# A row sort in which GpSimd makes a sixth of the upper payload words

## The reference

```python
idx = jnp.argsort(vf, axis=-1)                  # 3136 values of each channel
vs = jnp.take_along_axis(vf, idx, axis=-1)
gat = lambda t: jnp.take_along_axis(t.reshape(b, c, hw), idx, axis=-1)
out1 = _reshape_attn(gat(q1), gat(k1), vs, temperature, True)
out2 = _reshape_attn(gat(q2), gat(k2), vs, temperature, False)
inv = jnp.argsort(idx, axis=-1)
out1 = jnp.take_along_axis(out1, inv, axis=-1)  # and out2
```

## Time and profile before

| | us |
|---|---|
| median of 3 runs | 15142.0 (15140.57 to 15142.44) |
| the profiled execution | 15131.19 |
| its span | 15129.3 |
| VectorE busy | 13763.9 (91%) |
| ScalarE busy | 7104.4 (47%) |
| TensorE busy | 6739.8 (45%) |
| GpSimd busy | 6003.8 (40%) |

### The profile page before, as it was taken

One profiled execution on the slowest core, in us unless ns is written; L12 is line 12 of the kernel. 1 busy time (PEld: TensorE's weight loads), 2 busy tenths in 40 slices (PEclk: granted clock), 3 DMA queues, 4 the chain that ended last, 5 costly groups with the idle time before them and its releaser, 6 DMA issues. The chain is left out here.

```text
span 15129.3 us, 121619 instructions
## 1 busy us (share of the span) xinstructions
PE 6739.8 (45%) x42188; PEld 2753.7 (18%) x42188; DVE 13763.9 (91%) x8241; ACT 7104.4 (47%) x6587; POOL 6003.8 (40%) x4372
## 2 busy tenths in 40 slices
PE   4777744481025625714814723833732015433310
PEld 2443421120012211211201211211211002111100
DVE  4777778899999999999999999999999999989978
ACT  0000003355575565565565566566566555444443
POOL 0000000066666666666666666666666640000000
PEclk8888877795557857856956966966866557666655
DMA  1554553110001000100100100100100001221232
GB/s 33 123 134 109 131 118 76 55 43 13 12 12 35 27 12 30 32 12 30 31 12 26 36 12 23 38 12 12 45 17 12 33 29 53 84 66 54 77 76 66
DMA packets 343162, 699.24 MB, mean 46 GB/s; under 512 B 71581, under 2 KB 275582, under 8 KB 331702
## 3 DMA queue, kind: packets, MB, share of 16 engines
q1 hardware_dynamic: 342518, 691.17, 17.1%
HBM read 480.98 MB, written 209.95 MB: 46 GB/s over the span
## 5 line engine op out<-in xcount | busy, mean ns | idle before, releaser
L1183 DVE COPY_PREDICATED arena<-psum,arena 128x4096 f32<-128x4096 uint32 (+26 forms) x1456 | 4009.6, 2771 | 46.4 <-ACT psum L1143 45.8
L1190 DVE COPY_PREDICATED arena<-psum,arena 128x4096 f32<-128x4096 uint32 (+26 forms) x1456 | 3969.2, 2742 | 42.0
L1009 PE MATMUL psum<-arena,wt 128*32 128x448 f32 x31360 | 3224.9, 573 | 1239.5 <-DMA arena<-xpad 698.8
L1108 POOL TENSOR_TENSOR arena<-arena 128x1024 int32<-128x1024 int32 (+26 forms) x1456 | 2077.7, 1433 | 3061.6 <-DVE arena L1175 3058.2
L1094 POOL TENSOR_TENSOR arena<-arena 128x1024 bf16<-128x1024 f32 (+26 forms) x1456 | 1975.6, 1363 | 3284.0 <-SPq L267 3081.3
L1131 ACT ACTIVATE arena<-arena 128x4096 f32<-128x4096 f32 (+26 forms) x1456 | 3071.7, 2126 | 71.1 <-DVE arena L1190 38.0
L1151 ACT ACTIVATE masks<-psum 128x512 fp8e4<-128x512 f32 (+27 forms) x1256 | 923.6, 736 | 3563.6 <-DVE arena L1190 3562.5
L1100 POOL TENSOR_TENSOR arena<-arena 128x1024 int32<-128x1024 int32 (+26 forms) x1456 | 2006.1, 1384 | 0.0
L1009 PEld LDWEIGHTS psum<-arena,wt 128*32 128x32 f32 x31360 | 1039.5, 115 | 3427.5 <-issue 2326.4
L1399 PE MATMUL psum<-ident,arena 128*112 128x128 f32 x896 | 197.1, 386 | 2443.1 <-ACT arena L1318 1879.8
L1175 DVE TENSOR_TENSOR arena<-arena 128x1024 f32<-128x1024 f32 (+26 forms) x1456 | 1163.4, 812 | 100.4 <-POOL arena L1100 100.4
(11 more groups left out here) (131 smaller groups left out, 7837.8 us busy)
## 6 DMA issues: line engine op xcount, KB each, us to landing
arena<-xpad SPq DMA_DIRECT2D x896, 108.5 KB, 2.3
arena<-simd SPq DMA_DIRECT2D x416, 210.0 KB, 4.3
arena<-simd SPq DMA_DIRECT2D x416, 196.0 KB, 4.4
xpad<-arena SPq DMA_DIRECT2D x8, 1924.0 KB, 14.6
arena<-in_x SPq DMA_DIRECT2D x8, 1568.0 KB, 7.3
x3d<-arena SPq DMA_DIRECT2D x8, 1568.0 KB, 5.3
prodd<-arena SPq DMA_DIRECT2D x8, 1568.0 KB, 5.1
arena<-prodd SPq DMA_DIRECT2D x8, 1568.0 KB, 14.0
```

Of the source, the lines that this page charges most:

```text
L1009: last = nc.tensor.matmul(psum[C * b:C * b + C, n % C_BANKS, 0:CROWS * W], wt[:, g, C * w:C * w + C], cx[i % 2][b][:, y0:y0 + CROWS, x0:x0 ...
L1108: last = nc.gpsimd.tensor_tensor(hi, packed_view(stmp, here, piece, 1), lo, ALU.subtract)
L1183: last = nc.vector.copy_predicated(lo, wide_mask(q, k, piece, here), hi)
L1190: last = nc.vector.copy_predicated(hi, wide_mask(q, k, piece, here), packed_view(ptmp, here, piece, NP))
```

## The change

A share (POOL_SHARE = 0.16) of the pairs of each lot is cut off at its upper end (`cut_piece`, `shared_lot`), at a boundary of a block, of a run or of 8 elements where one is within a sixteenth of the lot. The table SHARED holds for each level and lot the pieces kept and the pieces given. For the kept ones all stays as it was. For the given ones:

- GpSimd forms the integer sum of the lower and upper payload words into `ptmp` (`pay_sums`), ahead of the masked copy, and afterwards writes the upper words as that sum less the new lower ones (`pay_uppers`).
- ScalarE's `keep_pay` and VectorE's `upper` leave them out. VectorE's `lower` still covers all pairs.

New waits: `pay_sums` waits for `upper` and `pay_uppers` of the level before, `pay_uppers` for the lot's `lower`, `keep_pay` for `pay_uppers` of the level before, `lower` for `pay_sums`. GpSimd's order is written anew: difference and sum of a level are made one level ahead, lot by lot, behind the upper keys of the same lot; only at LAST_LEVEL both lots wait until the level before is through.

```diff
+POOL_SHARE = 0.16
+def cut_piece(piece, x, slack):
+    base, nb, sb, j0, ng, sg, w, d = piece
+    block, n = ng * w, size(piece)
+    for unit in (block, w, 8, 1):
+        if w % unit and unit < w:
+            continue
+        c = min(n, max(0, round(x / unit) * unit))
+        if abs(c - x) <= slack:
+            break
...
+def shared_lot(rows):
+    total = sum(size(piece) for piece, _ in rows)
+    x, slack = total * (1 - POOL_SHARE), total / 16
+    kept, given = [], []
+    for piece, _ in rows:
+        low, high = cut_piece(piece, min(size(piece), max(0, x)), slack)
+        kept += low
+        given += high
+        x -= size(piece)
+    return kept, given
...
+            def pay_sums(q, k):
+                if q:
+                    pool.wait_ge(d_hi[k], q)
+                    pool.wait_ge(k_pu[k], q)
+                    if k or q == LAST_LEVEL:
+                        pool.wait_ge(d_hi[1 - k], q)
+                        pool.wait_ge(k_pu[1 - k], q)
+                for piece, here in shared_rows(q, k, 1):
+                    lo, hi = pair_views(pay[b].bitcast(i32), piece, NP)
+                    last = nc.gpsimd.tensor_tensor(packed_view(ptmp.bitcast(i32), here, piece, NP), lo, hi, ALU.add)
+                last.then_inc(k_ps[k], 1)
+
+            def pay_uppers(q, k):
+                pool.wait_ge(k_ps[k], q + 1)
+                pool.wait_ge(d_lo[k], q + 1)
+                for piece, here in shared_rows(q, k, 1):
+                    lo, hi = pair_views(pay[b].bitcast(i32), piece, NP)
+                    last = nc.gpsimd.tensor_tensor(hi, packed_view(ptmp.bitcast(i32), here, piece, NP), lo, ALU.subtract)
+                last.then_inc(k_pu[k], 1)
+
+            def prepare(q, k):
+                differ(q, k)
+                sums(q, k)
+
+            for k in range(2):
+                prepare(0, k)
+                pay_sums(0, k)
             for q in range(SR):
-                if q == LAST_LEVEL:
-                    uppers(q - 1, 1)
-                differ(q, 0)
-                sums(q, 0)
-                if q and q != LAST_LEVEL:
-                    uppers(q - 1, 1)
-                differ(q, 1)
-                sums(q, 1)
-                uppers(q, 0)
-            uppers(SR - 1, 1)
+                ahead = q + 1 < SR and q + 1 != LAST_LEVEL
+                for k in range(2):
+                    uppers(q, k)
+                    if ahead:
+                        prepare(q + 1, k)
+                    pay_uppers(q, k)
+                    if ahead:
+                        pay_sums(q + 1, k)
+                if q + 1 == LAST_LEVEL:
+                    for k in range(2):
+                        prepare(q + 1, k)
+                        pay_sums(q + 1, k)
...
             def keep_pay(q, k):
                 if q:
                     act.wait_ge(d_hi[k], q)
+                    act.wait_ge(k_pu[k], q)
                     if k or q == LAST_LEVEL:
                         act.wait_ge(d_hi[1 - k], q)
-                for piece, _, here in lot_rows(q, k):
+                        act.wait_ge(k_pu[1 - k], q)
+                for piece, here in shared_rows(q, k, 0):
...
             def lower(q, k):
                 dve.wait_ge(d_cp[k], q + 1)
+                dve.wait_ge(k_ps[k], q + 1)
                 dve.wait_ge(d_mw[k], q + 1)
...
             def upper(q, k):
                 dve.wait_ge(d_lo[k], q + 1)
-                for piece, _, here in lot_rows(q, k):
+                for piece, here in shared_rows(q, k, 0):
```

More of the change, by code:

```diff
@@ L179, with group @@
 assert all(lot_size(q, 0) <= lot_at(q, 1) for q in range(len(ROW_LOTS)))
+POOL_SHARE = 0.16
[8 more added lines that the diff above has]
+            break
+    b, rest = divmod(c, block)
+    g, i = divmod(rest, w)
+    low, high = [], []
+    def group(into, lo, hi):
+        if lo < hi:
+            into.append((base + b * sb, 1, sb, j0 + g * sg + lo, 1, 0, hi - lo, d))
+    if b:
+        low.append((base, b, sb, j0, ng, sg, w, d))
+    if g:
+        low.append((base + b * sb, 1, sb, j0, g, sg, w, d))
+    group(low, 0, i)
+    if i:
+        group(high, i, w)
+    first = g + (i > 0)
+    if rest and first < ng:
+        high.append((base + b * sb, 1, sb, j0 + first * sg, ng - first, sg, w, d))
+    done = b + (rest > 0)
+    if done < nb:
+        high.append((base + done * sb, nb - done, sb, j0, ng, sg, w, d))
+    assert sum(map(size, low)) == c and sum(map(size, low + high)) == n
+    return low, high
+def shared_lot(rows):
[8 more added lines that the diff above has]
+    return kept, given
+SHARED = [[shared_lot(rows) for rows in lots] for lots in ROW_LOTS]
 for q, (first, second) in enumerate(ROW_LOTS):
+    assert all(kept and given for kept, given in SHARED[q])
     assert sum(size(x) for x, _ in first + second) == ROW_NET[q][2]
@@ L1029, in c_scalar @@
                         yield
-        k_df, k_sm, k_up = ([sem(f"k_{n}{k}") for k in range(2)] for n in ("df", "sm", "up"))
+        k_df, k_sm, k_up, k_ps, k_pu = ([sem(f"k_{n}{k}") for k in range(2)] for n in ("df", "sm", "up", "ps", "pu"))
         d_mw, d_mcp, d_cp, d_lo, d_hi = ([sem(f"d_{n}{k}") for k in range(2)] for n in ("mw", "mcp", "cp", "lo", "hi"))
@@ L1035, in program @@
         d_mst = [sem(f"d_mst{i}") for i in range(4)]
-        d_sems = [*k_df, *k_sm, *k_up, *d_mw, *d_mcp, *d_cp, *d_lo, *d_hi, *d_lv, *d_mst]
+        d_sems = [*k_df, *k_sm, *k_up, *k_ps, *k_pu, *d_mw, *d_mcp, *d_cp, *d_lo, *d_hi, *d_lv, *d_mst]
         pmask = psum[:, 4:8, :].rearrange("p k n -> p (k n)")
@@ L1043, in lot_rows, with shared_rows @@
                 yield piece, at, here
+                here += size(piece)
+        def shared_rows(q, k, part):
+            kept, given = SHARED[q][k]
+            here = lot_at(q, k) + (sum(map(size, kept)) if part else 0)
+            for piece in (kept, given)[part]:
+                yield piece, here
                 here += size(piece)
```

## The result

The changed kernel takes 15766.8 us in the median of 4 runs (15764.8 to 15768.1), the kernel before beside it 15142.2 (15140.6 to 15143.1): the ratio is 1.0414, with a 95% interval of 1.0397 to 1.0430. It is 625 us slower; the forecast was 15,790. The profiled execution took 15764.8 us, its span is 15762.9.

A forecast was written before the change was run, and what follows sets the result against it. GpSimd was to replace VectorE as the bound: 1082 work + 44 handovers + 100 and 6 port - 9 overlap + 25 edges = 1248 us per sort against 1166.6, so 650 us slower: 15,790 us, range 15,370 to 16,080.

The forecast's parts named there:

- What goes away: VectorE's upper payload copies lose 66,308 words per sort: 69 us per sort, 550 us in eight sorts.
- GpSimd's new operations: Two integer payload operations per given piece, 356 per sort at 0.98 us each: 349 us per sort.
- The port: SBUF access shared by GpSimd and VectorE's two-input operations: GpSimd loses 100 us per sort to key minima, 6 to attention.
- The handovers: GpSimd operations waiting for the subtraction before them: two per lot at 0.14 us, 44 us per sort.
- The edges: GpSimd idle at each sort's start, at LAST_LEVEL and in the last level: together 25 us per sort.
- The whole: GpSimd's total need per sort: 1248 us, against 1166.6 us per sort before the change.
- Rival 1: VectorE stays the bound, paying for the port, with payload words at 1.67 ns: near 15,440 us; chance 0.20.
- Rival 4: Met waits cost 0.14 us each and minima take the port for their full 1.21 us: near 16,340; chance 0.06.
- The new wait of ScalarE: ScalarE's payload copy waits for GpSimd's payload subtraction, holding back mask words queued behind it: given no cost.
- VectorE's slices: Sign in the profile after: VectorE's busy tenths per slice in the sorts fall from 9 to 8.
- rival 2: The two engines don't hinder each other when loaded: 15,015 us, or 14,590 with cheap payload words; together chance 0.08.
- The rule of the Trainium skill: Whichever engine starts first keeps the shared ports for the whole instruction, 1.21 us per minimum: sum about 190 us higher.

The follow-up runs named there:

- the run without payload work: Changed kernel with all waits and order kept, but GpSimd's payload sums and subtractions left out: 14598.0 us, ratio 0.9640.
- the run with one input: Changed kernel with the key minimum replaced by an in-place reduction over one element, reading one arena operand, so nothing is sorted: 15107.9 us, ratio 0.9979.
- the run with the mask words first: Changed kernel with ScalarE's mask words written ahead of its payload copy in each lot: 15745.3 us, ratio 1.0401.
- the share of 0.12: Changed kernel with a share of 0.12 instead of 0.16 and nothing else: 15429.0 us, ratio 1.0191.
- 0.08: Changed kernel with a share of 0.08 instead of 0.16: 15111.7 us, ratio 0.9983.
- the masked key copy with 0.12: Changed kernel with the key minimum made a copy under the PSUM mask, mask words ahead of ScalarE's payload copy, share 0.12: 15068.6 us, ratio 0.9954.

## Why the prediction was right

The forecast and the result differ by 23 us, and it is right by its steps, not only by its sum. GpSimd's needs per sort are, in the sum and as measured, 1082 and 1082 us of work, 44 and 40 of handovers, 97 and 91 of the port (the attention's 6 lie in the measured 1082), 25 and 34 of edges and waits. That the differences of -4, -6 and +9 cancel is luck, but a small one:

- **What goes away:** 550 us by the sum, 543 by the run without payload work (565 by the upper copies' group, of the changed kernel).
- **GpSimd's new operations:** 0.98 us each in the sum, 0.991 and 0.989 in the run with one input, 351 us per sort by that run ((1404.3 + 1400.9)/8) for 349. With the key operations GpSimd is busy for 8656.04/8 = 1082 us per sort there, overlapping records counted once:

```profile
3021.00:12328.00 9307.00, 3977.61 (x30128) 1475.96 (x30128) 8559.15 (x4964) 5114.76 (x5088) 8656.04 (x7216) 0.70 0.07 23
```

- **The port:** 100 us per sort for the key minima, 6 for the attention's operations, less 9. The one-input run shows 91 for the key minima, from GpSimd's side; the attention's part is in both runs and not in this difference. Its two-input operation (L1468, L1373 before) takes 1285 ns in the one-input run and 711 in the kernel before, so it too meets the port. The forecast of VectorE's side was loose ("1.2 us and more" for the mean; 1.37).
- **The handovers:** 44 us per sort in the sum. What GpSimd's idle time before the differences and the payload sums has left, once what the waits name is taken off, is 3245.8 - 3058.0 - 27.1 = 161 us (27.1 us is named as issue among its waits) and 252.3 - 94.4 = 158 us, together 40 us per sort.
- **The edges and GpSimd's other waits:** 25 us in the sum. The stretch has 1247 us per sort, GpSimd is busy for 1173, and less the 40 the rest is 34. Of these 25 are the waits for VectorE that the groups name ((84.6 + 94.4 + 23.8)/8).
- **The whole:** 1248 us per sort, 1247 measured.

Rival 1, VectorE as the bound with cheap payload words, fell with the price of a payload operation: 0.99 us and not 0.80 (0.18 us + 372 x 1.67 ns). Rival 4, at 16,340, needed another 44 us of handovers and 24 of the port per sort; with 40 and 91 us measured, neither is there.

Three points were wrong and hidden by the sum. The new wait of ScalarE was given no cost; VectorE waits 307 us behind it, and it is nearly harmless only because GpSimd is slower still: the run with the mask words first gave back 22 us. VectorE's slices were to fall from 9 to 8 and stay at 9, since its longer minima count as busy. And rival 2, "the two engines don't hinder each other", was priced at 15,015; the one-input run is that case and took 15,108. The step that failed there is "GpSimd's need is the time per sort": at nine tenths GpSimd also waited for single lots (1163 us per sort instead of 1151; 32 of them are waits for VectorE, where 25 were allowed for all edges), and VectorE waited 535 us for mask words. Whether these waits for mask words cost time there wasn't tried: no run has one input and the mask words first. The same step made the estimate for the share of 0.12 miss. The one for 0.08 missed by another term, the port waits of VectorE, 38 us per sort and not up to 98. The step held in the changed kernel, by the four terms above.

The rule of the Trainium skill (SBUF — State Buffer, Who interferes with whom) that the pair of ports is kept for the whole instruction was weighed at 190 us more. In the measured sum there is no room for it: 91 us per sort are 0.89 us for 1024 pairs on average, the few minima that met an idle GpSimd included, where the minimum alone takes 1.21. The contention is there, as the Trainium skill says, and GpSimd's loss is smaller than the recorded duration of the minimum.

## What to carry to other kernels

Before work is moved to GpSimd, look at which VectorE instructions beside it read two operands from SBUF: each waits for a running GpSimd instruction and then blocks the next. Here this cost 39 us while GpSimd was six tenths busy and 659 us at nine tenths. Count GpSimd's time, these handovers and the waits on its own results in one sum, and leave it a clear margin below VectorE: where the two were about equally long (0.12, and 0.16 with one input), each waited for the other and the time lay above what either engine alone was estimated to need. Where a mask lies in PSUM, a masked copy can stand for a minimum, and GpSimd's times beside it were those without the port (1433 ns instead of 1535 for the key subtraction); but look at the spacing of its words first.

## What the runs showed of the hardware

The masked copy of single words depends on their spacing. Four-word payload elements cost 1.09 ns a word. 1024 keys in runs of four and more take 1.30 to 1.46 us, but keys in pieces of width 1 or 2 cost some 2.4 ns each (2494 ns for 1022). The reduction and the minimum over the same 1022 keys take 1.20 and 1.21 us:

```profile
L1269 DVE TENSOR_REDUCE arena<-arena 128x1022 f32<-128x1022 f32 x16 | 19.3, 1203 | 0.0
```

They slow down too at some of the first levels, but less: 512 single keys that stand four words apart take 1.65 us in the one-input run (at 3057.29), where the masked copy takes 2.56 (at 3058.22). What limits the copies wasn't tried, and it was not expected. At 125 ns a copy over the 0.9 us assumed, 1456 copies make some 180 us, of the 254 us by which the masked key copy with 0.12 missed its estimate; that all of it lay in the path is not shown, for giving the minimum back to these pieces saved only 56 us.
